# A feed-forward/attention kernel: the norm's low pieces and last router logits moved, and attention's first projections, mask and layout moved into the end of the first feed-forward

## The reference

```python
x = x + 0.5 * ffn(layernorm(x))
x = x + attention(layernorm(x))
x = x + 0.5 * ffn(layernorm(x))
# attention: 16 heads of 16 columns, causal mask, softmax, output projection
# ffn: shared silu(x w1) * (x w2) @ w3 with 1024 hidden columns, plus a router (sigmoid of 16 logits,
#      the two best experts of each row) and 16 experts of 256 hidden columns, each weighed by its score
```

## Time and profile before

| what | us |
| --- | --- |
| median of 3 runs | 1528.1 |
| lowest and highest | 1527.01, 1534.37 |
| the profiled execution | 1521.6 |
| its span in the trace | 1519.9 |
| TensorE busy in it | 1445.3 (95%) |

### The profile page before, as it was taken

The page is one execution under the profiler, slowest core; times in us unless marked ns, Lnnn a source line. Parts: engine busy times, 40 slices in busy tenths (PEclk is TensorE's granted clock), DMA queues, the critical chain, the costliest instruction groups (busy, mean ns, idle before and its releaser), DMA issues. The chain is left out here.

```text
span 1519.9 us, 28879 instructions
## 1 busy us (share of the span) xinstructions
PE 1445.3 (95%) x8935; PEld 1161.6 (76%) x8968; DVE 962.7 (63%) x2019; ACT 666.3 (44%) x1347; POOL 589.2 (39%) x832
## 2 busy tenths in 40 slices
PE   4999999999989987999999999979999999999998
PEld 2688878888878875666667666658888888888887
DVE  6678865555545666776677676635776455555566
ACT  3534444343433434665655665553322334433332
POOL 6528830233323024463464464321188333333100
PEclk9999999999999998999999999979999999999999
DMA  9898998535386955445554554536464534356941
GB/s 339 306 334 281 326 333 337 175 106 183 104 274 205 304 168 110 93 114 139 138 130 116 131 123 114 156 121 227 174 243 148 204 120 146 105 184 219 305 132 56
DMA packets 176534, 285.82 MB, mean 188 GB/s; under 512 B 20738, under 2 KB 125698, under 8 KB 176146
## 3 DMA queue, kind: packets, MB, share of 16 engines
q1 hardware_dynamic: 134642, 206.31, 43.2%
q0 software_dynamic: 19104, 56.64, 10.2%
q10 hardware_dynamic: 22656, 21.11, 4.8%
HBM read 144.20 MB, written 109.84 MB: 167 GB/s over the span
## 5 line engine op out<-in xcount | busy, mean ns | idle before, releaser
L1615 PE MATMUL f_bank<-f_xparts,f_sw 128*128 128x512 f32 x1536 | 378.2, 396 | 3.7 <-DVEq L1546 3.2
L1615 PEld LDWEIGHTS f_bank<-f_xparts,f_sw 128*128 128x128 f32 x1536 | 284.9, 191 | 59.2 <-DVEq L1546 3.3
L1107 POOL DMA_INDIRECT outputs_by_choice<-f_yr,f_home x160 | 153.4, 959 | 364.4 <-DVE f_yr L1570 298.1
L2314 DVE TENSOR_REDUCE at_mx<-at_ps 128x1 f32<-128x384 f32 (+3 forms) x352 | 213.6, 632 | 110.6 <-PE at_ps L2443 103.8
L2208 ACT ACTIVATE at_pT<-at_ps 128x512 f32<-128x512 f32 (+1 forms) x352 | 194.0, 559 | 70.2 <-PE at_ps L2459 61.5
L2124 POOL TENSOR_SCALAR_AFFINE_SELECT at_pT<-at_pT 128x128 f32<-128x128 f32 (+2 forms) x352 | 123.5, 359 | 220.2 <-ACT at_pT L2208 215.6
L1065 POOL DMA_INDIRECT rows_by_slot<-f_xq,slot x128 | 149.8, 1171 | 121.6 <-issue 70.0
L2459 PE MATMUL at_ps<-fa_qT,fa_kT 98*128 98x256 f32 (+3 forms) x512 | 171.7, 388 | 4.9 <-DMA fa_qT<-at_mT 2.5
L1461 DVE TENSOR_TENSOR f_hid<-f_sil,f_bank 128x512 f32<-128x512 f32 x128 | 87.8, 686 | 131.4 <-PE f_bank L1615 106.8
L1559 DVE TENSOR_TENSOR f_sil<-f_sil,f_bank 128x256 f32<-128x256 f32 x160 | 67.3, 421 | 161.4 <-ACT f_sil L1210 157.3
L1190 ACT CAST f_hparts<-f_hid 128x512 fp32r<-128x512 f32 x128 | 79.4, 620 | 200.3 <-DVE f_hid L1461 178.8
(11 more groups left out here) (250 smaller groups left out, 2464.4 us busy)
## 6 DMA issues: line engine op xcount, KB each, us to landing
f_ring<-weights_in_parts SPq DMA_DIRECT2D x32, 768.0 KB
weights_in_parts<-fa_whi SPq DMA_DIRECT2D x30, 768.0 KB, 7.8
f_rawx<-rows_by_slot ACTq DMA_DIRECT2D x152, 128.0 KB
at_whi<-weights_in_parts SPq DMA_DIRECT2D x16, 768.0 KB
fa_ew<-in_L_ffn_routed_w_dram SPq DMA_DIRECT2D x42, 256.0 KB
rows_by_slot<-zero POOLq DMA_DIRECT2D x10, 1024.0 KB, 20.4
f_xq<-xn_rows POOLq DMA_DIRECT2D x32, 256.0 KB
fa_ew<-outputs_by_choice SPq DMA_DIRECT2D x8, 1024.0 KB, 9.5
```

Source lines behind the costliest of these rows:

```text
L1107: nc.gpsimd.indirect_dma_start(dram.yk, bass.IndirectOffsetOnAxis(ap=home[:, i:i + 1], axis=0), yr[:, i % 4, :], None).then_inc(y_st[i % 4 ...
L1615: ins = pe.matmul(ps[j % 2][:, :], sw12[:, wp, k, w, j * P:(j + 1) * P], xparts[:, u, xp, k, :], start=(i == 0), stop=(i == 3 * KD - 1))
L2314: v.tensor_reduce(own, ps1[i % RING1][:, 0:heads * w].rearrange("p (j a x) -> p j a x", a=min(heads, 2), x=w), AX.X, ALU.max).then_inc(mx_ ...
```

## The change

It has two parts, one at each end of the first feed-forward.

In the front, GpSimd's constants for routing come first, before its first `deviation`. `low_piece` now also waits for `normed`, so that it starts when the normalizing of the chunk before is over. The low part of the value weights moves to chunk 4 and `low_weights` follow the same chunks as before. TensorE's `turn_logits` moves ahead of `route`, each chunk has columns of its own in `psL`, and one copy takes six chunks of logits at the end. The logits of the last two chunks are turned after the first `up` of the feed-forward, out of rows that ScalarE copies there, and the sigmoid comes in step 1 instead of ahead of step 0; `routing` starts one step later.

At the end of the first feed-forward, the projections of attention's first two groups come between the last `up` and the two last `down` (the banks `psR` and `psC`); ScalarE and VectorE split them into `p0` and `p1`; GpSimd makes the mask and clears the first two slots of `kT` there; SyncE and GpSimd lay the first group out. The second group is laid out at the start of attention by SyncE and ScalarE. The last chunk's `residual` and its store move into attention.

```diff
-                dve.wait_ge(a_hi, 2 * j + 2)
+                dve.wait_ge(a_hi, 2 * j + 3)
...
-                if c >= 5:
+                if c == 4:
+                    dve.wait_ge(a_hi, 1)
+                    nc.vector.tensor_tensor(att.wv[:, 1], att.wraw[:, :, 2], att.wv[:, 0], ALU.subtract
+                                            ).then_inc(a_lo, 1)
+                elif c >= 5:
                     low_weights(c - 5)
             normalize(z.NC - 1, z.NC // 2 - 1, 1, False)
-            logits(z.NC - 4)
             low_weights(2)
             low_weights(3)
-            dve.wait_ge(a_hi, 4 * KD + 1)
-            nc.vector.tensor_tensor(att.wv[:, 1], att.wraw[:, :, 2], att.wv[:, 0], ALU.subtract).then_inc(a_lo, 1)
-            logits(z.NC - 3)
-            logits(z.NC - 2)
-            logits(z.NC - 1)
+            dve.wait_ge(logit, z.NC - 2)
+            n = (z.NC - 2) * CT * E
+            nc.vector.tensor_copy(g.logits[:, 0:n], psL[:, 0:n])
...
                 deviation(c, c % 2)
+                pool.wait_ge(normed, c)
                 low_piece(c - 3)
+            pool.wait_ge(normed, z.NC)
             for i in range(z.NC - 3, 6):
                 low_piece(i)
...
             for c in range(2, z.NC):
                 turn(c, c % 2, False)
+                turn_logits(c - 2, c % 2)
                 route(c - 1, 1 - c % 2)
-                turn_logits(c - 2, c % 2)
             route(z.NC - 1, 1)
-            turn_logits(z.NC - 2, 0)
-            turn_logits(z.NC - 1, 1)
...
-                logit_rows(c - 1)
+                if c < z.NC - 1:
+                    logit_rows(c - 1)
                 if c == 3:
                     act.wait_ge(a_in, 48)
                     nc.scalar.mul(att.wraw[:, :, 0], att.wraw[:, :, 0], QSCALE).then_inc(a_scaled, 1)
                     act.wait_ge(a_scaled, 1)
-                elif c >= 4:
-                    k, half = (c - 4) // 2, (c - 4) % 2
+                    nc.scalar.copy(att.wv[:, 0], att.wraw[:, :, 2]).then_inc(a_hi, 1)
+                for j in {4: (0, 1), 5: (2,), 6: (3,)}.get(c, ()):
+                    k, half = j // 2, j % 2
                     for i in range(2):
                         nc.scalar.copy(columns(att, 0, k, i, half), given(att, k, i, half)).then_inc(a_hi, 1)
-                    if c == 7:
-                        nc.scalar.copy(att.wv[:, 0], att.wraw[:, :, 2]).then_inc(a_hi, 1)
-            logit_rows(z.NC - 1)
...
+def lay_keys(eng, sem, att, s, parts, part, r):
+    src, k = parts[:, part, :].bitcast(F32), att.kT[:, s].bitcast(F32)
+    for a in range(2):
+        to = 32 * r + HEAD * a
+        lo = GROUP_ROWS + 32 * a
+        eng.dma_start(k[to:to + HEAD, a:GROUP:2, :], src[lo:lo + 32, :]).then_inc(sem, 16)
+def lay_queries(eng, sem, att, s, parts, part, r):
+    q = att.qT[:, s].bitcast(F32)
+    eng.dma_start(q[32 * r:32 * r + 32, :, :], parts[:, part, :].bitcast(F32)[0:GROUP_ROWS, :]).then_inc(sem, 16)
+def lay_half(eng, sem, att, s, parts, part):
+    if part == 0:
+        lay_queries(eng, sem, att, s, parts, 0, 0)
+        lay_keys(eng, sem, att, s, parts, 0, 0)
+    else:
+        lay_keys(eng, sem, att, s, parts, 1, 1)
+def lay_other(eng, sem, att, s, parts, part):
+    if part == 0:
+        lay_queries(eng, sem, att, s, parts, 0, 1)
+        lay_keys(eng, sem, att, s, parts, 0, 2)
+    else:
+        lay_queries(eng, sem, att, s, parts, 1, 2)
...
+                if not exact and c == NC - 1:
+                    sp.wait_ge(a_clear, 2)
+                    sp.wait_ge(acc_st[0], 32)
+                    sp.wait_ge(p_hi, 1)
+                    for part in range(2):
+                        if part == 1:
+                            sp.wait_ge(p_lo, 1)
+                        lay_half(sp, g.laid[0], att, 0, att.p0, part)
...
+                pool.wait_ge(summed, 6)
+                pool.sem_inc(g.held, 1)
+                for s in range(2):
+                    nc.gpsimd.memset(att.kT[0:ROWS, s].bitcast(F32), 0.0).then_inc(a_clear, 1)
+                pool.wait_ge(a_clear, 2)
+                pool.wait_ge(acc_st[0], 32)
+                pool.wait_ge(p_hi, 1)
+                for part in range(2):
+                    if part == 1:
+                        pool.wait_ge(p_lo, 1)
+                    lay_other(pool, g.laid_p, att, 0, att.p0, part)
...
+                nc.scalar.copy(rows_l, pre.psE[0:E]).then_inc(rows_in, 1)
...
+                elif s == 15:
+                    for G in range(2):
+                        act.wait_ge(p_full, G + 1)
+                        nc.scalar.copy((att.p0, att.p1)[G][:, 0, :], (psR, psC)[G][:]).then_inc(p_hi, 1)
...
-                    if exact and n == 7:
+                    if n == (7 if exact else 1):
                         act.wait_ge(logit_in, 1)
...
+                    if not exact and n == 0:
+                        dve.wait_ge(rows_turned, 1)
+                        v.tensor_copy(g.logits[:, (NC - 2) * CT * E:], psC[:, 0:2 * CT * E]).then_inc(logit_in, 1)
...
+                elif s == 15:
+                    for G in range(2):
+                        dve.wait_ge(p_hi, G + 1)
+                        v.tensor_tensor((att.p0, att.p1)[G][:, 1, :], (psR, psC)[G][:], (att.p0, att.p1)[G][:, 0, :],
+                                        ALU.subtract).then_inc(p_lo, 1)
...
+                    elif c == 0 and j == 0:
+                        pe.wait_ge(rows_in, 1)
+                        for i in range(2 * CT):
+                            ins = pe.transpose(psC[:, i * E:(i + 1) * E], rows_l[:, i // CT, i % CT * P:(i % CT + 1) * P],
+                                               g.ident[0:E, 0:E])
+                        ins.then_inc(rows_turned, 1)
...
+                    if not exact and last and j == z.JS - 1:
+                        pe.wait_ge(a_lo, KD)
+                        pe.wait_ge(a_w_in, 32)
+                        for G in range(2):
+                            i = 0
+                            for xp, wp in ((0, 0), (0, 1), (1, 0)):
+                                for k in range(KD):
+                                    ins = pe.matmul((psR, psC)[G][:], att.wqk[:, wp, k, G, :], att.xnT[:, 1, xp, k, :],
+                                                    start=(i == 0), stop=(i == 3 * KD - 1))
+                                    i += 1
+                            ins.then_inc(p_full, 1)
...
-        return ours(i + AHEAD, 0, TG) if s == AT_PROJ else None
+        return ours(i + AHEAD, MADE, TG) if s == AT_PROJ else None
...
+            for part in range(2):
+                lay_half(sp, laid[1], att, 1, att.p1, part)
+            sp.wait_ge(last_sum, CT)
+            sp.dma_start(rows(dram.x1, NB_ - 1), pre.last_rows).then_inc(g.last_st, 16)
...
+                    if c == 1:
+                        pool.wait_ge(laid[1], 16 * LAID)
...
+            pool.wait_ge(g.laid_p, 16 * 4)
+            pool.sem_inc(laid[0], 16 * 4)
...
+            pool.sem_inc(cleared, MADE)
+            for s in range(MADE, KEEP):
                 p.memset(kT[0:ROWS, s].bitcast(F32), 0.0).then_inc(cleared, 1)
+            p.tensor_copy(pick[:], g.ident[0:2, 0:2].rearrange("p (a o) -> p a o", o=1).to_broadcast([2, 2, CHUNK])
+                          ).then_inc(picked, 1)
             p.memset(va[:, :, :, :, 1:2 * DK:2], 1.0).then_inc(va_ones, 1)
...
+            act.sem_inc(hi_done, MADE)
+            for part in range(2):
+                lay_other(act, laid[1], att, 1, att.p1, part)
...
+            for t in range(CT):
+                rows_t = pre.last_rows[:, t, :]
+                v.scalar_tensor_tensor(rows_t, pre.last_out[t], 0.5, rows_t, ALU.mult, ALU.add).then_inc(last_sum, 1)
```

118 lines of the change are left out of this document (61 added, 57 removed).

## The result

| what | before | after |
| --- | --- | --- |
| median of 6 runs, us | 1530.2 | 1520.44 |
| lowest and highest | 1527.01, 1534.37 | 1519.05, 1521.64 |
| the profiled execution | 1521.6 | 1521.64 |
| its span | 1519.9 | 1519.9 |

The recorded ratio of the runs is 0.9949, 95% interval 0.9929 to 0.9969: the change saves 0.3 to 0.7%, about 7.8 us. (The two medians alone are 9.8 us apart, ratio 0.9936, inside the same interval.) So about two thirds of the 12.0 us forecast came. The two profiled executions have the same span: that of before is a fast one of its kind, 8.6 us under its median.

The account below looks back on a forecast made before the run. The prediction took TensorE's standstill in two serial stretches, the front and the seam around the first feed-forward, as the bound. Seam 10.0 plus front 2.0 made 12.0 us, from 1528.1 to 1516.1, range 1511 to 1523.

Parts of the forecast that it names:

- The front: From the start to the first feed-forward's first `up`: 2.0 us saved, with 3.5 and nothing as the other cases.
- One of the two adds gets in, the other waits for the piece of 2.35 us: Front, VectorE's low parts behind chunk 5: the pair takes 2.4 us instead of 0.48, so chunk 6 is normalized no earlier.
- the case that both get in: Front: both low-part adds get in ahead of GpSimd's piece each time, and the front saves 3.5 us.
- The small transposes: Feed-forward's first step: eight small transposes cost 0.8 us, during which `up` of step 1 waits.
- The seam: Between the last `down` of the first feed-forward and attention's first scores: 10.0 us saved, bounds 7 and 12.5.
- score to third projection: Start of attention on TensorE: first score at 566.4, third projection at about 570.5 instead of 580.52.
- with TensorE last at 562.7 and the same step of about 2.4 us: Step from the first feed-forward into attention: about 2.4 us behind TensorE's end, so attention begins at 565.1.
- a barrier that waits for GpSimd's copies: Seam: one of two reasons, beside the crowded landing, given for the lower bound of 7 us of gain.
- That cover is almost gone, and up to 1 us may be lost there: Early attention: GpSimd's normalizing of the second chunk ends near 577.9, TensorE's turn is at 578.6; up to 1 us lost.
- Rival 2: At the seam value product, scores and third projection run at the feed-forward's clock; gain 14 to 16 us, chance 0.10.
- Rival 4: Start of attention: slower, as GpSimd's normalizing of the second chunk also waits for the second group's copies; chance 0.03.
- rival 1: Seam: layout lands late, first scores at 569 to 570, front brings nothing; gain 4 to 9, about 1521.5, chance 0.18.

Follow-up runs that it names:

- act_lays_again: The changed kernel with ScalarE instead of GpSimd issuing the first group's four layout copies, repeated on another chip; 1513.75 us, ratio 0.9922 to the kernel before.
- front_transfers: The version with ScalarE's copies, plus four 2 KB GpSimd transfers in the first stage (the norm); 1514.66 us, ratio 0.9934 to the kernel before.
- early_gpsimd_dma: The kernel before, plus four 128 KB GpSimd transfers to spare DRAM some 14 us ahead of the first feed-forward's end; 1518.73 us, ratio 0.9977.
- act_lays: The changed kernel, but ScalarE instead of GpSimd issues the first group's four layout copies; 1513.64 us, ratio 0.992 to the kernel before.
- late_compute: The kernel before, plus one small 128x4 GpSimd operation about 2 us ahead of the first feed-forward's end, no transfer; 1528.62 us, ratio 1.0028.
- late_gpsimd_dma: The kernel before, plus four 128 KB GpSimd transfers to spare DRAM late in the first feed-forward; 1532.38 us, ratio 1.0057.
- after_again: The changed kernel run once more, nothing altered, on the same chip as the runs beside it; 1516.21 us, ratio 0.9977 to the kernel before.
- compute_behind: The changed kernel, plus one small 128x4 GpSimd operation behind its four late layout copies; 1516.67 us, ratio 0.9969 to the kernel before.
- landed_first: The changed kernel, but GpSimd waits at the first feed-forward's end until its four layout copies have landed; 1524.34 us, ratio 0.9987 to the kernel before.

## Why the prediction came out as it did

The recorded 1516.1 lies 4.3 us under the result, inside its range. Two of its terms were wrong, with opposite signs, and the larger one by 8 us. That the time is still inside the range is in part luck: the stages as measured give 5.3 to 5.7 us, which from the 1528.1 of the forecast is 1522.4 to 1522.8, just inside its end at 1523, and the reason isn't one that the range was drawn for.

**The front, 2.0 forecast, 3.4 to 3.8 measured.** The step that failed: "One of the two adds gets in, the other waits for the piece of 2.35 us". In this trace both adds get in, both times: the pairs start 0.1 us ahead of the end of the normalizing (35.54 and 39.51), and GpSimd's pieces 0.3 us behind the pairs (35.82 and 39.79), as the second add has just begun. GpSimd wasn't free much earlier: its 1/sqrt(variance) of the next chunk ended at 35.85, and the second piece's high part came from ScalarE at 39.65. So it is a matter of tenths of a microsecond, and in act_lays_again and front_transfers, where the first pair was late, it was held as forecast and the first `up` came at 53.6 and 53.0; the forecast had 52.4. Where a piece was there first, the low parts were held (1.64 us at 30.88, 1.51 at 46.25), as the earlier trace rows had it. My text gave 3.5 for the case that both get in. So the last store is issued at 47.24 (48.3 forecast), SyncE's wait for it ends 3.3 us later (3.2 forecast), and the next stage begins on SyncE at 50.78 and on TensorE at 51.27, 1.28 us behind its last product. The small transposes took 0.67 us (0.8 forecast).

**The seam, 10.0 forecast, 1.9 measured.** Most terms held. The projections took 2.91 us, attention's first row to first score 1.4 (1.3 forecast), score to third projection 3.7 (4.1). One product list was misread, ahead of the prediction and in it: the projections stand between the two last `down` (553.81 and 557.99), only one is behind them, and TensorE was done 1.1 us earlier against the last `up` than forecast (5.6 us behind its end, not 6.7). What failed is "with TensorE last at 562.7 and the same step of about 2.4 us". The step did not keep that length: it took 10.4 us from the end of the others. I had taken 2.4 us from an execution in which GpSimd's list had ended at 536.36 (and counted from VectorE's end; SyncE ended later, at 561.38). From its last operation to attention, over the kernels:

| kernel | GpSimd ends | its drain ends | others end | attention | since GpSimd | since others |
| --- | --- | --- | --- | --- | --- | --- |
| before | 536.36 | 545.20 | 561.38 | 563.43 | 27.1 | 2.05 |
| early_gpsimd_dma | 540.37 | 549.52 | 554.47 | 556.54 | 16.2 | 2.07 |
| act_lays | 546.56 | 555.40 | 562.03 | 564.16 | 17.6 | 2.13 |
| late_compute | 556.97 | 565.80 | 560.75 | 567.46 | 10.49 | 6.7 |
| late_gpsimd_dma | 556.48 | 565.62 | 557.88 | 567.28 | 10.80 | 9.4 |
| after | 560.32 | 569.46 | 560.75 | 571.17 | 10.85 | 10.4 |
| after_again | 554.91 | 564.04 | 555.35 | 565.76 | 10.85 | 10.4 |
| compute_behind | 551.89 | 561.05 | 552.08 | 562.76 | 10.87 | 10.7 |

GpSimd's drain reaches 8.8 to 9.2 us past its last instruction in every row. Two clocks run to attention, 2.1 us from the last of the other engines and 10.5 to 10.9 from GpSimd (its drain, and 1.7 for barriers and clearing), and the later one counts. Before, GpSimd's would have allowed attention at about 547, hidden behind the last chunk. The change moved GpSimd's last instruction from 536 to 560 and brought it out. I had named "a barrier that waits for GpSimd's copies" and bounded it by 7 us of gain: the right place, the wrong mechanism (in landed_first the copies had landed and the step was as long), and a bound with no row behind it. The trace of the kernel before held the drain of 9.4 us at 535.8; I read 3.81 us of TensorE's idle time as a fact about the step, without asking when each engine had got there.

**Given back later.** "That cover is almost gone, and up to 1 us may be lost there": since attention starts late, GpSimd's normalizing ends at 584.5 and TensorE waits 1.24 us for it at 584.66. With ScalarE's copies it does not wait (577.62).

**The clock.** The granted clock of the stretch from the last `down` to the first score is 0.68 again; behind it the third projection ran at the upper level (1.64 us), and behind the wait for GpSimd the fourth at the lower (2.70 against 1.66 before). Rival 2 didn't come. Rival 4 neither; rival 1 gave about the right time for the wrong reason, since no score waited for a landing.

**Between.** From first to last `up` the feed-forward took 491.6 (early_gpsimd_dma) to 502.1 us (act_lays), in no order that goes with the kernels. Of the front's 3.4 us, 2.1 are left at the last `up` of the profiled pair (551.06 against 553.12); the rest is within that spread and isn't explained further. It is also why whole times differ from the stages' sum: 3.4 to 3.8 and 1.9 make 5.3 to 5.7, inside both intervals of the change.

**Left open.** Why GpSimd's drain is long at the end of a feed-forward. It needs no late transfer (late_compute) and none of its own in flight (landed_first), it isn't the clearing of semaphores (0.78 to 0.83 us, in front of attention alone), and not the length of the list (attention's is the longest, and its drain reaches 0.07 us past it). What is left is what the feed-forwards have and the other stages lack: GpSimd issues 170 transfers in the first and 160 in the second, 144 of them indirect in each. Four direct transfers more make the drain 0.3 us longer, late, early or in the norm, but ten fewer in the second feed-forward don't make it shorter, so it is no plain sum over them. A stage with many direct or a few indirect ones wasn't tried.

## What to carry to other kernels

A barrier's price isn't one number: read for each engine when its list ended and how long its drain lasts, both in the trace, and before giving an idle engine work at a stage's end, ask what its idle time was hiding. Try the cheapest thing that could cause a stall (here a 0.22 us operation) before blaming the expensive one (four transfers). Where one engine is slow to leave a stage, give its last work to another: the same four issues on ScalarE made the seam 8 us shorter.

## What was not expected of the hardware

GpSimd's drain at the end of the first feed-forward reached 8.8 to 9.2 us past its last instruction, whatever that instruction was, and attention began 10.49 to 10.87 us behind that instruction in the five rows of the table in which GpSimd was late, against 2.05 to 2.13 us behind the last of the other engines where it was early. At the end of the norm the drain reached 0.06 us past it, and 0.4 with four transfers in the stage. The Trainium skill, page "VectorE: DVE Perf Modes", section "The DRAIN you can't avoid", has drains of about 12 ns on all five engines for those that frame a program. Inside this program the other four engines' drains around the clearing of semaphores agree (7 to 19 ns); GpSimd's do not, 46 and 287 ns there and 9 us at the feed-forward's end.
